# A two-layer graph network on one core: the first stage's products taken four at a time instead of two

## The reference, cut to what matters

```
h    = h @ W + b
nh   = h / max(norm(h), eps)
cos  = nh @ nh.T                    # 1024 x 1024
h    = (edge_weight * cos) @ h      # relu after the first two
```

## Time and profile before

| | |
|---|---|
| median of three runs | 3010.84 us |
| profiled execution, its own time | 3018.62 us |
| its span | 3016.8 us |
| first stage (`layer0`) in the span | from the start to about 1866 us |
| TensorE busy over the span | 2784.0 us (92%) |
| VectorE busy | 2277.1 us (75%) |
| ScalarE busy | 1251.4 us (41%) |
| GpSimd busy | 1082.2 us (36%) |
| mean granted TensorE clock | 0.975 of full |
| DMA, share of 16 engines | 46.8% |

### The profile page before, as it was taken

How to read it: one execution, slowest core, us unless ns; L and a number is a source line. 1 busy time by engine, 2 the same in 40 slices (tenths; PEclk the granted TensorE clock), 3 DMA queues, 4 the chain that set the end, 5 groups by cost and what they waited for, 6 DMA issues and landing times. The chain is left out here.

```text
span 3016.8 us, 41011 instructions
## 1 busy us (share of the span) xinstructions
PE 2784.0 (92%) x13446; PEld 1740.0 (58%) x13446; DVE 2277.1 (75%) x6124; ACT 1251.4 (41%) x3652; POOL 1082.2 (36%) x493
## 2 busy tenths in 40 slices
PE   6988999998999998899998997799999979999997
PEld 4655656655555655556655564455555545555786
DVE  4788998888988898898888886766566524676567
ACT  2544541545541554541554530233332224443564
POOL 4534333434333232321000000776666612443661
PEclk9999999999999999999999998899999989999998
DMA  6446336446327345326214102355554516996653
GB/s 215 134 136 206 105 99 213 137 130 210 109 84 227 113 133 192 105 62 190 91 57 164 60 15 98 128 212 215 191 188 181 189 70 242 396 395 270 241 200 126
DMA packets 304077, 492.27 MB, mean 163 GB/s; under 512 B 18544, under 2 KB 196080, under 8 KB 303856
## 3 DMA queue, kind: packets, MB, share of 16 engines
q1 hardware_dynamic: 303856, 489.57, 46.8%
HBM read 422.38 MB, written 67.11 MB: 162 GB/s over the span
## 5 line engine op out<-in xcount | busy, mean ns | idle before, releaser
L478 POOL TENSOR_SCALAR a_AT<-a_ats 128x512 uint8<-128x512 f32 x256 | 504.2, 1974 | 871.2 <-DMA a_ats<-in_adjT 809.3
L538 PE MATMUL a_acc<-a_ew,a_Hr 128*128 128x512 f32 x1536 | 796.0, 600 | 3.1 <-ACT a_hT L626 3.1
L717 DVE TENSOR_TENSOR a_ew<-adj,a_cos 128x512 f32<-128x512 f32 x768 | 522.6, 681 | 146.4 <-PE a_cos L531 145.2
L529 PE MATMUL a_cos<-a_nh 128*128 128x512 f32 x768 | 447.3, 582 | 2.4 <-DVE a_nl L709 2.4
L1286 POOL TENSOR_TENSOR b_dsum<-adj 128x1024 f32<-128x1024 f32 x16 | 141.9, 8870 | 662.2 <-DVE adj L1240 662.2
L538 PEld LDWEIGHTS a_acc<-a_ew,a_Hr 128*128 128x128 f32 x1536 | 292.3, 191 | 73.3 <-DVE a_ew L717 3.6
L640 ACT ACTIVATE a_vr<-a_D,a_sm_b,a_sm_sc 128x128 f16<-128x128 f32 x560 | 210.6, 456 | 246.0 <-DVE a_sm_b L766 245.4
L531 PE MATMUL a_cos<-a_nh,a_nl 128*128 128x512 f32 x768 | 306.3, 399 | 0.0
L530 PE MATMUL a_cos<-a_nl,a_nh 128*128 128x512 f32 x768 | 305.9, 398 | 0.0
L1130 PE MATMUL b_acc<-adj,b_h 128*128 128x512 f32 x512 | 224.3, 596 | 22.5 <-DVE adj L1240 22.5
L1290 POOL TENSOR_TENSOR b_dsum<-b_dsum,adj 128x1024 f32<-128x1024 f32 x96 | 225.8, 2352 | 14.1 <-POOL b_dsum L1290 0.5
(11 more groups left out here) (204 smaller groups left out, 4756.6 us busy)
## 6 DMA issues: line engine op xcount, KB each, us to landing
adj<-in_adjT SPq DMA_DIRECT2D x108, 1024.0 KB, 12.7
adj<-in_adjT SPq DMA_DIRECT2D x128, 512.0 KB, 5.8
a_ats<-in_adjT SPq DMA_DIRECT2D x256, 256.0 KB, 3.4
a_af<-in_adj SPq DMA_DIRECT2D x256, 256.0 KB, 3.4
scr_keep<-a_kp SPq DMA_DIRECT2D x128, 128.0 KB, 1.8
b_kp<-scr_keep SPq DMA_DIRECT2D x16, 1024.0 KB, 8.2
c_zi<-scr_z SPq DMA_DIRECT2D x32, 512.0 KB, 6.1
c_ai<-scr_ag SPq DMA_DIRECT2D x32, 512.0 KB, 7.0
```

The costliest lines, as they stand in the source:

```text
L478: e.tensor_scalar(AT[i][:, 4 * h:4 * h + 4, blk(k)].bitcast(U8), ats[h][:], 0.0, ONE8, ALU.is_gt, ALU.mult).then_inc(T["at"], 1)
L529: e.matmul(cos[j][:], n[:, blk(k)], n[:, half(j)], start=True, stop=False)
L538: e.matmul(acc[j][:], Hr[u % 2][:, k, :], ew[idx % 3][:], start=(k == 0), stop=(k == NK - 1)).then_inc(E["agg"], 1)
L717: e.tensor_tensor(ew[idx % 3][:], adj[g % 2][:, k, half(j)], cos[j][:], ALU.mult).then_inc(E["ew"], 1)
```

## The change

In `layer0_plan` the `cos` and `agg` parts of two steps are taken together: at an even step the list has `cos(idx + 2)`, `cos(idx + 3)`, `agg(idx)`, `agg(idx + 1)`, and at an odd step neither. Both `evac` parts stand at the unit's step 14. All other parts keep their step. `ew` has four buffers in place of three, since `cos(idx + 3)` now stands ahead of `agg(idx)`. `hT` becomes one buffer in place of two, with one new wait, at the very last unit.

```diff
-        if idx + 2 < 2 * NK * 3 * G:
-            out.append(("cos", idx + 2))
-        out.append(("agg", idx))
+        if idx % 2 == 0:
+            if idx + 2 < 2 * NK * 3 * G:
+                out += [("cos", idx + 2), ("cos", idx + 3)]
+            out += [("agg", idx), ("agg", idx + 1)]
         out.extend(agenda.pop(here, []))
         flush()
-        if here >= 14:
-            out.append(("evac", u, here - 14))
+        if here == 14:
+            out += [("evac", u, 0), ("evac", u, 1)]
...
-        hT = [P.sb(f"hT{i}", [128, N]) for i in range(2)]
+        hT = P.sb("hT", [128, N])
...
-        ew = [P.sb(f"ew{i}", [128, 512]) for i in range(3)]
+        ew = [P.sb(f"ew{i}", [128, 512]) for i in range(4)]
...
-                    e.matmul(acc[j][:], Hr[u % 2][:, k, :], ew[idx % 3][:], start=(k == 0),
+                    e.matmul(acc[j][:], Hr[u % 2][:, k, :], ew[idx % 4][:], start=(k == 0),
...
                     e.wait_ge(E["agg"], 16 * u + 15 + j)
-                    e.activation(hT[u % 2][:, half(j)], acc[j][:],
+                    if u + 1 == 3 * G and j == 0:
+                        e.wait_ge(E["tpost"], G - 1)
+                    e.activation(hT[:, half(j)], acc[j][:],
                                  ACT.Relu if UNITS[u][1] < 2 else ACT.Copy).then_inc(E["ev"], 1)
...
-                    e.tensor_tensor(ew[idx % 3][:], adj[g % 2][:, k, half(j)], cos[j][:], ALU.mult).then_inc(E["ew"], 1)
+                    e.tensor_tensor(ew[idx % 4][:], adj[g % 2][:, k, half(j)], cos[j][:], ALU.mult).then_inc(E["ew"], 1)
```

More of the change, by code:

```diff
@@ L509, in pe @@
                     for k in range(NK):
-                        t = e.matmul(pp[:, k, :], hT[g % 2][:, blk(k)], W[:, i, :], start=True, stop=True)
+                        t = e.matmul(pp[:, k, :], hT[:, blk(k)], W[:, i, :], start=True, stop=True)
                     t.then_inc(E["ph"], 1)
@@ L519, in pe @@
                     e.wait_ge(E["nl"], min(u + 2, 3 * G))
-                    transposes(lambda k: hT[UNITS[u][0] % 2][:, blk(k)], E["tpost"])
+                    transposes(lambda k: hT[:, blk(k)], E["tpost"])
                 elif kind == "cos":
@@ L604, in act @@
                         e.wait_ge(E["tpost"], g - 1)
-                    e.activation(hT[g % 2][:], flat2(pp), ACT.Relu).then_inc(E["relu"], 1)
+                    e.activation(hT[:], flat2(pp), ACT.Relu).then_inc(E["relu"], 1)
                 elif kind == "hb":
```

## The result

The changed kernel takes 3152.36 us (median of four runs, 3147.63 to 3158.28), against 3010.76 before (now of four runs too): a ratio of 1.0467, 95% interval 1.0441 to 1.0493, 141 us slower. The forecast was 3123, slower by 112. The profiled execution has a span of 3156.5 us, the granted clock over it is 0.968 (before 0.975).

A forecast was written before the change was run, and what follows sets the result against it. First-stage TensorE was taken to bound the kernel, waiting only for VectorE's and ScalarE's dilation answers. Terms -7 + 39 + 26 + 49 + 0 + 5 = +112 us gave 3131 profiled, 3123 as a median; range 3040 to 3195, forecast's own 3085 to 3160.

The forecast's parts named there:

- The path: First stage: products never wait; TensorE waits for VectorE's and ScalarE's answers to dilation matmuls; stage to end near 1978.
- Masks: Two masks in a pair, second's transposes bare behind VectorE's readings: +1.05 us in two thirds of 56 pairs, +39 us.
- Rounds: Rule then drops, no `ew` between: 4.3 us against 3.71, +0.45 for 108 rounds, +49 us, bounds 0 and 84.
- the wait on the cosine: Expected sign in the profile after: first cosine matmul (L529) waits tens of us for a late `ew`, against 0.0.
- Wides: Two wides in a pair, second waits 1.1 us for banks freed by `b1` and `v`: +26 us, bounds 10 and 35.
- Starts: Starts' `first`: even start loses a step's cover, odd one gains it: 0 us, bounds -30.8 and +13.
- Changes of kind: TensorE going from dilation matmul to cosine loses 0.06 us, 120 times fewer: -7 us, bounds 0 and 10 gained.
- the agenda: `ha` behind `lnc` waits for a ScalarE copy of 1.04 us, less covered: +5 us, bounds 0 and 15.
- Buffers: One `hT` and a fourth `ew` buffer: no new wait binds and none is removed, 0 us.
- The clock: Granted clock in the first stage, 0.99 before, expected to stay despite pauses of 0.5 to 1 us.
- a sign of being wrong: Granted clock under 0.97 in the first stage would show the prediction wrong.
- the clock rival: Mask stretches fall to 1.2 GHz, 56 x 3.1 = 174 us more, 3297 us; chance 0.04.

The follow-up runs named there:

- given back: Changed kernel with the old order in one kind of pair, time regained: 56 mask pairs 40 us, 32 wide 17, 140 rule 42, 55 start 26.
- 36 alone: Order of before, with the new order only in the 56 pairs whose two steps both hold a mask: 3053.19 us, ratio 1.0119.
- the shifted kernel: Changed kernel with every dilation stage one step later: 3190.08 us, ratio 1.0563; the kernel before, shifted likewise: 3033.5 us, ratio 1.0056.
- the four kinds back: Changed kernel with the old order in rule, start, two-mask and two-wide pairs (283 of 384): 3033.24 us, ratio 1.0051.
- the 38 pairs: Order of before, new order only in pairs with a wide and no further wide, or without any stage: 3020.57 us, ratio 1.0026.
- the four variants with one kind back: Changed kernel with the old order in one kind of pair: masks 3116.01 us, wides 3138.48, rule pairs 3115.46, starts 3128.58.

## Why the prediction was right

**The path.** Right: the products did not wait before, so more cover ahead of them bought nothing, and everything lost is in the first stage. Three quarters of it, 102.5 of 139 us, are waits of TensorE on VectorE and ScalarE, as forecast; the rest is not (see the clock). The stage ends at 2005; 1978 was forecast.

**Masks**, forecast 39: 40 given back, 36 alone. The pair was put at 5.17 and takes 5.24. The last two masks of the old trace, the one place where it showed the bare case, gave this almost exactly. That two thirds of the 56 pairs would pay it was a guess for which no row stood, and it came out.

**Rounds**, 49: 42 given back; a bare round 4.3 forecast, 4.37 measured, and the wait on the cosine, "tens of us", is 37.7. The empty 0.6 us on VectorE is shown as the cause by the shifted kernel, whose undisturbed round is back at 3.68.

**Wides**, 26: 17. The waits are those worked out (on `b1`, then on `v`), but in the pair shown they come to 0.75 us of idle time and not 1.1, and a part of them stood in front of a wait for the drops that was there anyway.

**Starts**, 0 with +13 as the bound: 26. This is the term that was most mis-sized, and its bound was wrong. The step said that VectorE's work is back to back either way, and gave a bare `first` 0.3 us. It forgot that in the new order two `ew` instead of one stand between two starts' operations on VectorE just where TensorE comes directly; in the pair shown the wait is 2.32 us. The terms that are not starts sum to nearly the forecast, 39 + 26 + 49 - 7 + 5 = 112 against 141 - 26 = 115, but in part by luck: rounds and wides came out 16 us below, the pairs outside the four kinds 17 above.

**Changes of kind**, -7, and the agenda, +5: not seen singly. `ha` behind `lnc` waits 9.1 us, forecast in kind (L511 on L606). The 101 pairs outside the four kinds cost 15 together, where these two terms come to -2; with the four kinds back 10.0 us of waits on a late `ew` are left, which the prediction looked for in the rounds alone. A gain of 7 from fewer changes between dilation and cosine shows in no run.

**Buffers**, 0: 0.

**The clock.** I expected it to stay, which put it at nothing in the sum; that was wrong. In the stage it goes from 0.99 to 0.97, just at the bound that I had called a sign of being wrong. Over the span (1 - 0.968) x 3156.5 - (1 - 0.975) x 3016.8 = 26 us of full speed more are withheld, and since the later stages have 0.96 in both kernels, that is in the first. What such time costs, the scatter within one kernel shows. Of the twelve runs of the 38 pairs, the two at 0.977 took 3015.58 and 3018.48 us, the two at 0.973 took 3027.33 and 3029.60: about 12 us more withheld, 11 us longer. So, as an estimate from these runs, most of the 26 us are in the loss, as the likely bulk of the 36.5 us for which TensorE is busy longer. No run parts the clock from the waits. The shares above contain it: over the runs the granted clock averages 0.968 after, 0.969 to 0.971 in the four variants with one kind back, and 0.975 with all four back.

Behind the wait of 2.32 us shown above, the windows of the kernel after (the column behind POOL is the granted clock):

```profile
870.00:877.00 7.00, 4.40 (x30) 2.60 (x29) 5.78 (x10) 4.11 (x8) 0.00 (x0) 1.00 0.22 61
877.00:881.00 4.00, 4.00 (x9) 2.23 (x8) 2.94 (x6) 0.00 (x0) 1.92 (x1) 0.57 0.74 221
881.00:888.00 7.00, 7.00 (x38) 4.25 (x36) 5.15 (x18) 1.54 (x5) 2.11 (x1) 1.00 0.00 0
```

For most of 877 to 881 it is at 1.2 GHz, though TensorE is busy throughout, and at 2.4 GHz again after. Just before, TensorE had waited 0.28 and 2.32 us with only one start's small counts between. The Trainium skill ("TensorE: Matmul & The Clock Gate", section on why this matters for your kernels) warns that pauses between bursts of matmuls bring the lower clock. The trace agrees in kind, though the single wait here is shorter than the gaps that the page warns of. It is not the stretch of several hundred microseconds that the clock rival priced at 174 us, but some short ones.

## What to carry to other kernels

When engines run one written order, ask of each regrouping not what it brings together but what it leaves bare: list every instruction that waits for an answer, with what now stands between question and answer, on both engines. A buffer with two readings that must end before the next write (here 1.05 us a pair) is free only as long as other work lies between. Look in the old trace for the one place where the case already occurs, often the last iteration; here it gave the price of a pair to 0.07 us. And count for the answering engine too what newly stands ahead of its answer: that was the largest missing term. Two more: where a trace is cut into pieces can make a gain out of nothing, so compare at more than one cut; and waits of 2 us on TensorE can cost once more behind them, by the clock.

## What the runs showed of the hardware that was not expected

The granted clock fell to 0.57 in the 4 us behind waits of 0.28 and 2.32 us (7 us with TensorE busy for 4.40), and was back at 1.00 in the 7 us after. The mean over the stage went from 0.99 to 0.97 while its waits grew from 109 to 212 us in all; the longest single one is 5.5 us after and 3.3 before. I had looked only at pauses of 0.5 to 1 us. With the mask pairs alone in the new order (53.7 us of waits in 98 places) the clock stayed, at 0.977. And a microsecond of withheld clock cost about a microsecond in the scatter of one kernel's runs (0.977 to 0.973, 11 us).
